# Row maxima of a 16-head attention: 512-key spans for 400-key spans, and the turned maxima split on ScalarE and GpSimd instead of VectorE

## What is computed

```python
def _L0_xattn_ref(values, keys, query, Wv, Wk, Wq, Wo, bo):
    H, Dh = (NUM_HEADS, HEAD_DIM)
    v = (values @ Wv.T).reshape(N, -1, H, Dh)
    k = (keys @ Wk.T).reshape(N, -1, H, Dh)
    q = (query @ Wq.T).reshape(N, -1, H, Dh)
    energy = jnp.einsum('nqhd,nkhd->nhqk', q, k)
    attn = jax.nn.softmax(energy / jnp.sqrt(jnp.float32(EMBED_DIM)), axis=3)
    out = jnp.einsum('nhql,nlhd->nqhd', attn, v).reshape(N, -1, H * Dh)
    return out @ Wo.T + bo
```

## Time and profile before

| | |
|---|---|
| median of three runs | 3645.14 us |
| the profiled execution | 3645.8 us, span 3644.0 us |
| TensorE busy in the span | 3391.9 us (93%) |
| VectorE busy | 2494.9 us (68%) |
| ScalarE busy | 1520.4 us (42%) |
| GpSimd busy | 226.7 us (6%) |
| mean granted TensorE clock | 0.966 of full speed |

### The profile page before, as it was taken

One profiled execution on the slowest core, in us unless ns is written; L12 is line 12 of the kernel. 1 busy time (PEld: TensorE's weight loads), 2 busy tenths in 40 slices (PEclk: granted clock), 3 DMA queues, 4 the chain that ended last, 5 costly groups with the idle time before them and its releaser, 6 DMA issues. The chain is left out here.

```text
span 3644.0 us, 63094 instructions
## 1 busy us (share of the span) xinstructions
PE 3391.9 (93%) x21900; PEld 2020.3 (55%) x21900; DVE 2494.9 (68%) x5808; ACT 1520.4 (42%) x2718; POOL 226.7 (6%) x251
## 2 busy tenths in 40 slices
PE   8979999999999999769977999977999999999999
PEld 5643222222222222258854545546989898989888
DVE  4538888888888888250013444438888888888885
ACT  4534777777777777412211222212222222222221
POOL 0021100000000000030000000000000000000000
PEclk9987999999999999879988999998999999999999
DMA  5687646465554642141120212112000000000000
GB/s 213 240 253 94 82 64 84 67 78 73 74 78 67 85 63 33 52 174 38 37 86 30 90 59 71 60 55 103 9 13 10 12 10 12 10 12 10 12 10 9
DMA packets 144167, 239.79 MB, mean 66 GB/s; under 512 B 22808, under 2 KB 100224, under 8 KB 143488
## 3 DMA queue, kind: packets, MB, share of 16 engines
q1 hardware_dynamic: 134768, 220.67, 28.6%
q0 software_dynamic: 4608, 12.59, 1.1%
q10 hardware_dynamic: 4624, 4.46, 0.4%
HBM read 170.38 MB, written 66.86 MB: 65 GB/s over the span
## 5 line engine op out<-in xcount | busy, mean ns | idle before, releaser
L656 DVE TENSOR_REDUCE at_pmax<-at_psm 128x2 f32<-128x800 f32 (+1 forms) x1024 | 968.1, 986 | 115.8 <-PE at_psm L504 94.0
L597 ACT ACTIVATE ring<-at_pss 128x512 f32<-128x512 f32 (+1 forms) x1664 | 865.2, 600 | 302.6 <-PE at_pss L518 298.3
L518 PE MATMUL at_pss<-at_qs,at_ks 99*128 99x512 bf16 (+1 forms) x1664 | 506.8, 386 | 8.0 <-ACT ring L597 6.5
L1659 PE MATMUL mt_psd<-mt_xl,mt_key_in 128*128 128x128 f32 x4096 | 491.1, 278 | 2.3 <-DMA mt_key_out<-m_out 2.3
L1659 PEld LDWEIGHTS mt_psd<-mt_xl,mt_key_in 128*128 128x128 f32 x4096 | 469.7, 193 | 3.7 <-DMA mt_key_out<-m_out 2.4
L1685 PE MATMUL mt_psu<-mt_key_out,mt_g 128*128 128x256 f32 x2048 | 447.4, 379 | 1.3 <-DVE mt_g L1895 1.3
L526 PE MATMUL at_pso<-ring,at_vw 128*32 128x512 f32 (+1 forms) x3328 | 444.1, 606 | 0.0
L1685 PEld LDWEIGHTS mt_psu<-mt_key_out,mt_g 128*128 128x128 f32 x2048 | 386.7, 190 | 52.6 <-DVE mt_g L1895 1.4
L502 PE MATMUL at_psm<-at_ks,at_qs 64*128 64x400 bf16 (+1 forms) x1024 | 340.1, 347 | 42.6 <-DVE at_pmax L656 18.9
L502 PEld LDWEIGHTS at_psm<-at_ks,at_qs 64*128 64x128 bf16 x1024 | 88.8, 93 | 467.0 <-DVE at_pmax L656 312.7
L504 PE MATMUL at_psm<-at_kh,at_qh 64*128 64x400 bf16 (+1 forms) x1024 | 339.8, 347 | 0.0
(11 more groups left out here) (218 smaller groups left out, 3781.7 us busy)
## 6 DMA issues: line engine op xcount, KB each, us to landing
at_ks<-k_dram SPq DMA_DIRECT2D x192, 200.1 KB, 6.7
k_dram<-pj_kp SPq DMA_DIRECT2D x24, 800.5 KB, 5.5
v_dram<-pj_v SPq DMA_DIRECT2D x8, 1664.0 KB, 9.1
at_vd<-v_dram SPq DMA_DIRECT2D x32, 416.0 KB, 10.7
pj_ctx<-ctxT SPq DMA_DIRECT2D x8, 1601.0 KB, 11.7
at_kh<-k_dram SPq DMA_DIRECT2D x128, 100.1 KB, 5.6
aw_ctxT<-ctxT SPq DMA_DIRECT2D x8, 1601.0 KB, 7.2
at_qs<-q_dram SPq DMA_DIRECT2D x192, 64.0 KB, 7.0
```

What stands on the lines that cost most here:

```text
L518: nc.tensor.matmul(ps_s[0:r, (NST * g + n) % SBANKS, :], ks[:, g, j, kt * P:kt * P + r], qs[:, g, j, :], start=True, stop=True).then_inc(s ...
L597: nc.scalar.activation(pr[0:r, (NST * g + n) % PRING, :], ps_s[0:r, (NST * g + n) % SBANKS, :], ACT.Exp, scale=SCALE).then_inc(expd, 1)
L656: nc.vector.tensor_reduce(pmax[:, 2 * p:2 * p + 2, q, c:c + 1], ps_m[:, n % MBANKS, :, 0:MSPANS[c][1]], AX.X, ALU.max).then_inc(m_red, 1)
L1659: ins = nc.tensor.matmul(ps_d[:, j % 2, y * P:y * P + P], key_in[:, k, j * YB + y, :], xl[:, s, k, :], start=k == 0, stop=k == KC - 1)
```

## The change

- A maxima job takes 512 keys: three full spans per head pair and query tile make 24 jobs. The 65 keys that remain (1536 to 1600) make one job per head pair for all four query tiles: eight matmuls of 65 columns side by side in one double bank, and one reduce of 2 x 4 x 65. That is 26 jobs per unit, exactly two per step.
- The two jobs of a step stand between the second and the third score (`BETWEEN = 2`); there are no third jobs. The two 65-key jobs are the last of a unit, in step 9. Eight jobs (`EARLY`) instead of nine are begun in steps 10 to 13.
- The turn moves to behind the first score of step 10, and the turned maxima go to a bank of the scores' ring `ps_s`: one of every 53 slots of the ring. The scores behind it wait one exponential more, and the third score after it waits for ScalarE's copy of the turned maxima (`m_copied`).
- ScalarE copies the turned maxima to SBUF, behind the first exponential of step 10; GpSimd makes the three bf16 parts from the copy with four instructions, behind `divide` in its order. VectorE's `split` is gone, and with it job 1's wait for `m_parts`.
- `invert`'s pieces stand ahead of jobs 14, 16 and 18 of 26.
- In the beginning: 26 jobs alternate with 26 key products, six key products follow alone, then two jobs of unit 1, the turn, and six more jobs. The bias is loaded ahead of `rows_out`. VectorE's and GpSimd's loops over units are written out.

```diff
-    MSPANS = [(a, n) for a, n in spans(KEYS - 1, 400)]
-    MSPANS = [(0, 401)] + [(a + 1, n) for a, n in MSPANS[1:]]
-    NM = len(MSPANS)
-    max_jobs = [(p, q, c) for p in range(HG // 2) for q in range(QT) for c in range(NM)]
+    MSPAN = 512
+    NFULL, REST = KEYS // MSPAN, KEYS % MSPAN
+    NM = NFULL + 1
+    max_jobs = [(p, q, c) for p in range(HG // 2) for q in range(QT) for c in range(NFULL)]
+    max_jobs += [(p, None, NFULL) for p in range(HG // 2)]
...
-    INVERT_IN, INVERT_AT = 3, (17, 18, 22)
+    INVERT_IN, INVERT_AT = 3, (14, 16, 18)
     TURN_AT = 10
-    THREE = (2, 3, 5, 7, 8, 11, 13)
-    BETWEEN = 3
+    BETWEEN = 2
...
+    def score_slot(u, n):
+
+        return (1 + u * (NST + 1) + n + (n > TURN_BEHIND)) % SBANKS
...
                     pe.wait_ge(m_red, u * NJ + n + 1)
-                    nc.tensor.matmul(ps_m[:, n % MBANKS, 0, 0:w], qs[0:MAX_ROWS, g, 2 * p, q * P:q * P + P],
-                                     ks[0:MAX_ROWS, g, 2 * p, a:a + w], start=True, stop=True)
-                    nc.tensor.matmul(ps_m[:, n % MBANKS, 1, 0:w], qh[MAX_ROWS:2 * MAX_ROWS, g, p, q * P:q * P + P],
-                                     kh[MAX_ROWS:2 * MAX_ROWS, g, p, a:a + w], start=True, stop=True).then_inc(m_mm, 1)
+                    for q, to, w in [(x, x * REST, REST) for x in range(QT)] if q is None else [(q, 0, MSPAN)]:
+                        nc.tensor.matmul(ps_m[:, n % MBANKS, 0, to:to + w], qs[0:MAX_ROWS, g, 2 * p, q * P:q * P + P],
+                                         ks[0:MAX_ROWS, g, 2 * p, a:a + w], start=True, stop=True)
+                        ins = nc.tensor.matmul(ps_m[:, n % MBANKS, 1, to:to + w],
+                                               qh[MAX_ROWS:2 * MAX_ROWS, g, p, q * P:q * P + P],
+                                               kh[MAX_ROWS:2 * MAX_ROWS, g, p, a:a + w], start=True, stop=True)
+                    ins.then_inc(m_mm, 1)
...
                 def turn_max(u):
 
                     pe.wait_ge(m_all, u + 1)
-                    nc.tensor.transpose(turned_at, nmax[:, :], t["ident"][:, :]).then_inc(m_turned, 1)
+
+                    if u:
+                        pe.wait_ge(expd, (u - 1) * NST + TURN_BEHIND + 2)
+                    nc.tensor.transpose(turned_at(u), nmax[:, :], t["ident"][:, :]).then_inc(m_turned, 1)
...
+                    behind = n - TURN_BEHIND
+
+                    if behind == 3:
+                        pe.wait_ge(m_copied, min(u + 2, UNITS))
+                    elif u == 0 and n == 2:
+                        pe.wait_ge(m_copied, 1)
+                    else:
+                        pe.wait_ge(expd, u * NST + n + 1 + (behind in (1, 2)))
...
                         for j in range(HG):
-                            maxima(j, kt)
+                            if j == BETWEEN:
+                                maxima(kt)
                             if kt < KT:
                                 scores(u, g, kt * HG + j)
                             elif nxt is not None:
                                 scores(u + 1, nxt[1], j)
-                        if nxt is not None and kt == TURN_AT:
-                            turn_max(u + 1)
+                            if kt == TURN_AT and j == 0 and nxt is not None:
+                                turn_max(u + 1)
...
+                        if n == TURN_BEHIND and u + 1 < UNITS:
+                            turned_out(u + 1)
...
+                def turned_out(u):
+
+                    act.wait_ge(m_parts, u + 1)
+                    act.wait_ge(m_turned, u + 1)
+                    nc.scalar.activation(mfull[:, :], turned_at(u), ACT.Copy).then_inc(m_copied, 1)
...
+                def split(u):
+
+                    me = Own(pool, own_split, u, 3)
+                    pool.wait_ge(m_copied, u + 1)
+
+                    pool.wait_ge(m_in, u * 48 + 1)
+                    gate(pool, t["pool_gate"])
+                    me.then(nc.gpsimd.tensor_copy(mpart[:, 0, :], mfull[:, :]))
+                    me.then(nc.gpsimd.tensor_tensor(mrest[:, :], mfull[:, :], mpart[:, 0, :], ALU.subtract))
+                    me.then(nc.gpsimd.tensor_copy(mpart[:, 1, :], mrest[:, :]))
+                    nc.gpsimd.tensor_tensor(mpart[:, 2, :], mrest[:, :], mpart[:, 1, :], ALU.subtract).then_inc(m_parts, 1)
```

More of the change, by code:

```diff
@@ L348, in attend_heads, with jobs_at, turn_slot @@
     NLOAD = 2 * len(Q_PART) + 2 * MAX_PARTS
-    INVERT_IN, INVERT_AT = 3, (17, 18, 22)
+    INVERT_IN, INVERT_AT = 3, (14, 16, 18)
     TURN_AT = 10
-    THREE = (2, 3, 5, 7, 8, 11, 13)
-    BETWEEN = 3
+    BETWEEN = 2
     NJ = len(max_jobs)
[L355 to L362, removed]
+    PER_STEP = NJ // KT
+    assert NJ == PER_STEP * KT and QT * REST <= MSPAN
+    EARLY = PER_STEP * (KT + 1 - TURN_AT)
+    TURN_BEHIND = TURN_AT * HG
+    def jobs_at(kt):
+        first = (kt - 1) * PER_STEP + EARLY
+        return [n % NJ for n in range(first, first + PER_STEP)]
+    def score_slot(u, n):
+        return (1 + u * (NST + 1) + n + (n > TURN_BEHIND)) % SBANKS
+    def turn_slot(u):
+        return ((u - 1) * (NST + 1) + TURN_BEHIND + 2) % SBANKS if u else 0
     with Stage(nc, "at") as st:
@@ L541, in unit, with maxima @@
                     nxt, over = ((b, x) if x < G else (b + 1, x - G) if b < last else None for x in (g + 1, g + 2))
-                    def maxima(place, kt):
+                    def maxima(kt):
                         ahead, v = (nxt, u + 1) if kt < TURN_AT else (over, u + 2)
                         if ahead is not None:
-                            for n in plan[kt].get(place, ()):
+                            for n in jobs_at(kt):
                                 max_product(ahead[0], ahead[1], v, n)
@@ L566, in unit @@
                             values(u, g, (kt - 1) * HG + j)
-                        maxima("values", kt)
                 last = B - 1
@@ L572, in _ @@
                     max_product(0, 0, 0, n)
-                max_product(0, 1, 1, 0)
-                turn_max(0)
-                for n in range(1, EARLY):
+                for n in range(NJ, MH * len(halves)):
+                    key_product(n)
+                for n in range(MBANKS):
                     max_product(0, 1, 1, n)
                 pe.wait_ge(k_out, len(halves))
+                turn_max(0)
+                for n in range(MBANKS, EARLY):
+                    max_product(0, 1, 1, n)
                 first_scores(0, 0)
@@ L652, in maxima @@
                             invert(behind, me, INVERT_AT.index(n))
-                        if n == 0 and before is not None:
-                            split(before, me)
+                        if n == 0:
+                            dve.wait_ge(m_all, u)
                         dve.wait_ge(m_mm, u * NJ + n + 1)
-                        nc.vector.tensor_reduce(pmax[:, 2 * p:2 * p + 2, q, c:c + 1], ps_m[:, n % MBANKS, :, 0:MSPANS[c][1]],
-                                                AX.X, ALU.max).then_inc(m_red, 1)
+                        heads, found = pmax[:, 2 * p:2 * p + 2, :, :], ps_m[:, n % MBANKS, :, :]
+                        if q is None:
+                            heads, found = heads[:, :, :, c], found[:, :, 0:QT * REST].rearrange("p j (q n) -> p j q n", n=REST)
+                        else:
+                            heads = heads[:, :, q, c:c + 1]
+                        nc.vector.tensor_reduce(heads, found, AX.X, ALU.max).then_inc(m_red, 1)
                     dve.wait_ge(m_red, (u + 1) * NJ + MBANKS)
+                    dve.wait_ge(m_turned, u)
                     nc.vector.tensor_reduce(nmax[:, :], pmax[:, :, :, :].rearrange("p j q c -> p (j q) c"), AX.X, ALU.max, negate=True).then_inc(m_all, 1)
-                OWN_MAX, OWN = 3, 3 + 2
-                maxima(0, Own(dve, own))
-                maxima(1, Own(dve, own), 0)
-                with dve.Fori(1, UNITS - 1) as u:
-                    me = Own(dve, own, u, OWN)
-                    me.n = OWN_MAX - OWN
-                    maxima(u + 1, me, u, u - 1)
-                me = Own(dve, own, UNITS - 1, OWN)
-                me.n = OWN_MAX - OWN
-                split(UNITS - 1, me)
+                OWN = 2
+                maxima(0)
+                maxima(1)
+                for u in range(1, UNITS - 1):
+                    maxima(u + 1, Own(dve, own, u - 1, OWN), u - 1)
+                me = Own(dve, own, UNITS - 2, OWN)
                 for u in range(UNITS - 2, UNITS):
@@ L720, in _ @@
                 spread(0, 1, False)
+                split(0)
                 add_bias()
-                with pool.Fori(1, UNITS // 2) as i:
+                split(1)
+                for i in range(1, UNITS // 2):
                     for s in range(2):
@@ L725, in _ @@
                         divide(2 * i + s - 2)
+                        split(2 * i + s)
                 for u in range(UNITS - 2, UNITS):
```

30 lines of the change are left out of this document (11 added, 19 removed).

## The result

The changed kernel takes 3562.42 us (median of four runs, 3561.29 to 3567.27) against 3644.63 us for the kernel before beside it. The ratio is 0.9778, 95% interval 0.9761 to 0.9795: 82 us less. Forecast were 3570.7 us, that is 74 less, with a range of 3549 to 3610. The profiled execution is the slowest of the four, 3567.27 us with a span of 3565.6.

The account below looks back on a forecast made before the run. TensorE sets the pace, losing 2.75 us per 37.39 us unit to waits for reduces. 34.02 + 0.02 + 0.2 + 0.72 + 0.05 = 35.0 per unit; -74.4 from 3645.8, median 0.7 lower: 3570.7 us, range 3549 to 3610.

Parts of the forecast that it names:

- The step: TensorE's step of four scores, two jobs and values: 2.617 us, thirteen of them 34.02 us per unit.
- No wait and no reserve: Chain through a bank: 2.85 us from the first job, next step's second job at 2.84, so no ordinary wait, no reserve.
- The rival of a longer chain: Each 1024-column reduce costs 0.05 us more than the slope says: 0.9 us per unit, 3599 us; chance 0.17.
- The 65-key jobs: Small pairs of 65 columns on TensorE: +0.02 us per unit, bounds +0.5 and -0.11 per job.
- The turn: Transpose between two scores on TensorE: 0.2 us per unit, bounded by 0.1 and 0.3.
- The inversion: `invert` on VectorE delays reduces: 0.46 us for the first transpose, 0.26 for the second, together 0.72 per unit.
- The boundary: Step where ScalarE also copies the sums: the fourth score waits for the first's exponential, 0.05 us per unit.
- The beginning: Stretch ahead of the first scores, with its jobs, key products and turn: -1 us, between -4 and +3.
- GpSimd: GpSimd's split of the turned maxima: four instructions of 0.5 us, 2.0 in all, hidden with 1.1 us of cover.
- late rows: GpSimd needs 1.28 us per instruction, so the next unit's first scores wait 2.0 us: 3633 us; chance 0.06.
- VectorE as the bound: Above 1.31 us between reduces, two don't fit a step; at 1.5 us the kernel takes 3703 us; chance 0.05.
- the wait only changes its name: Waits at the second job stay at 2.4 to 2.8 us per unit: 3640 to 3650 us; chance 0.04.

Follow-up runs that it names:

- the memsets: Changed kernel with a dead VectorE memset ahead of each step's second reduce: 3566.86 us with 64 columns, 3600.08 us with 192.
- second run of the changed kernel: The changed kernel itself, unaltered, measured again as base of the follow-ups: 3563.64 us, ratio 0.9778 to the kernel before.
- `BETWEEN = 3`: Changed kernel with each step's two jobs behind the third score instead of the second: 3585.32 us, ratio 0.9829 to the kernel before.
- bunched jobs: Changed kernel with a third job behind the values in steps 2, 5, 11 and one job less in 4, 7, 13: 3662.01 us.
- the run with three memsets: Changed kernel with three dead GpSimd memsets of 1024 columns ahead of each split from the third unit on: 3598.54 us, ratio 0.9874.

## Why the prediction was right, point by point

- **The step**: forecast 2.617, measured 2.61 to 2.64 in steps without extra work. Its terms hold: the second job 0.22 to 0.23 behind the first, the third score 0.31 behind that. It carries the gain, since 26 jobs spaced evenly leave no wait.
- **The reduce**: 1.22 by the slope of the earlier trace rows, measured 1.23; queued ones 2.36 - 1.23 = 1.13 apart, forecast 1.125. The step's idle time on VectorE is 0.26 to 0.35 in ordinary steps, forecast 0.37.
- **No wait and no reserve**: the reserve is shown to be nil by the memsets; in an ordinary step the second reduce ends at 809.66 and the next second job starts at 809.72. The rival of a longer chain had the right price, 0.9 per unit for a chain 0.1 longer (two reduces of 0.05 more), beside 1.18 measured for 0.15; the chain just wasn't longer.
- **The 65-key jobs**: forecast +0.02 per unit, measured -0.09 (step 9 takes 2.53). The truth lies between the nearest row that I took and the lower bound, which for two jobs was -0.22. TensorE's timeline of the changed kernel, the first two small pairs:

```profile
798.90 0.20 PE L511 MATMUL at_psm<-at_ks,at_qs 64*128 64x65 bf16 x1
798.90 0.20 PE L513 MATMUL at_psm<-at_kh,at_qh 64*128 64x65 bf16 x1
798.94 0.19 PE L511 MATMUL at_psm<-at_ks,at_qs 64*128 64x65 bf16 x1
```

  The two matmuls of a pair start together and pairs stand 0.03 to 0.04 apart, where a chain of matmuls that each load 128 rows needs 0.029 for one. But the second job's first pair starts at 799.13, 0.13 behind the last pair of the first job, so that one small job still takes 0.23, as a full one; what the 0.13 are, no run shows. The 0.09 come between the second job and the next score (0.23 instead of 0.32). The rule of the Trainium skill that was weighed there (TensorEngine Tiling, section Tiling Modes, Key Properties), that different tiles work in parallel, agrees with the pairs in these rows; the 7 us that it seemed to promise became 3.
- **The turn**: forecast 0.2, measured 0.11, near the lower bound: I took the middle where a row of it was missing.
- **The inversion**: forecast 0.46 + 0.26, measured 0.38 + 0.17 by the length of steps 5 and 7. The first transpose holds the next reduce up for 0.73 us (820.10 to 820.83) and not 0.83, which is that term's error; for the 0.09 of the second I have no row.
- **The boundary**: forecast 0.05, measured 0.05 (the first scores stand at 811.57 and 814.24, 2.67 apart).
- **Not in the sum**: step 11 is 2.69, 0.07 too long. Its second job starts 0.31 behind the first (804.15, 804.46) and waits for step 10's reduces, which start at 802.04, 0.50 behind their job instead of 0.43.

Together: 13 x 2.62 - 0.09 + 0.11 + 0.55 + 0.05 + 0.07 = 34.75, measured 34.77, forecast 35.0. The 0.23 too much are 7 us over 30 periods: the stretch from the first scores to the last values shrinks from 1193.4 us (316.00 to 1509.38) to 1115.1 in the second run of the changed kernel (317.29 to 1432.39), by 78.3 where 73.4 were forecast.

The forecast of 3570.7 is 8.3 us above the measured median. Of these the stretch explains 4.9, and the beginning, below, takes 2.3 back. Another 2.0 lie behind the attention, which the change doesn't touch (2134.6 us before, 2132.6 in the second run). The rest, some 3.6, is that the profiled execution used here took 3566.72 us and so stands above the medians; the forecast had allowed 0.7 for that. So part of how near the forecast came is luck: errors of both signs met.

- **The beginning**: forecast -1, measured +1.3 (first scores 316.00 before, 317.29). The turn does come earlier, 305.97 against 307.63, as the sum said. What failed is a time that it took as unchanged: the rows' three DMAs land 2.2 us after their issue before and 4.2 after. In the profiled run of the comparison they took 5.9 and the first scores came at 320.43; that is 3 of the 5 us by which this run stands above its median.
- **ScalarE's copy is free**: right, its cover is 0.2 us.
- **The exponential ahead of the third score** was taken to end before the score is due. It does, by 0.1 us, and only because the jobs stand in front. The prediction gave that cover no number, and so I didn't foresee the loss with `BETWEEN = 3`.
- **GpSimd**: forecast 2.0 us for the split, measured 1.62: two copies of 0.28 and two subtractions of 0.42. On VectorE the same four take 0.28, 0.28, 0.22 and 0.28. The rule of the Trainium skill that the prediction weighed (GPSIMD Engine Reference, Performance versus the Vector engine) is 1.96 times slower for an add with two inputs. For the subtractions of this small shape that is too high: 0.42 against 0.28, 1.5 times. The parts are issued at 803.97, 3.1 behind the first score of step 10 instead of 3.4, and the cover is 1.5 to 2.0.
- **The rivals**: late rows need a split over 1.5 us later than it is. VectorE as the bound, with a time above the kernel before, would have needed 1.42 us between reduces, against 1.13. That the wait only changes its name came true in two experiments, not in the change: with the turn and split moved but not the spans, and with bunched jobs.

## What to carry to other kernels

Where one engine feeds another through two buffers, a shorter chain per job isn't the first thing to look for: spread the jobs evenly over the steps first, since with the same work the bunched order was 95 us slower than the even one. Work out the chain through one buffer (start of the job to start of its reader, the reader's queue, its own time, release) and set it against the distance between the jobs that share the buffer; idle time of the reader is no reserve. A change of two parts can be worth more than the parts by themselves (81 us here against 63 and next to nothing), so run each alone, and look in the trace whether a run brings a wait of its own, as both did here. And put an engine's side work where it waits for its input anyway.

## What the runs showed of the hardware that I had not expected

- **The clock fell behind a single wait, and that cost more than the wait.** In the run with three memsets the granted clock went to half after one of the thirty waits, the longest, of 1.83 us; a timeline and a window behind it (columns as above):

```profile
993.45 1.01 PE L539 MATMUL at_pss<-at_qs,at_ks 99*128 99x512 bf16 x2 [1.83 <-issue]
...
996.32 1.94 PE L547 MATMUL at_pso<-ring,at_vw 65*32 65x512 f32 x8
```

```profile
995.00:997.00 2.00, 2.00 (x9) 0.33 (x10) 1.96 (x2) 1.15 (x3) 0.00 (x0) 0.50 0.08 18
```

  Matmuls ran at 1.2 GHz for some 10 us, and two steps took 4.74 and 4.77 us instead of 2.62, so the fall cost more than the wait itself. The wait of 1.52 us shown above had no such effect (clock 1.00 behind it). In the bunched run it happened twice between 400 and 1400 us, behind waits of 1.33 us (the values of 1.56 us in the timeline shown there) and 1.31 us, while a wait of 1.31 us at the same place in another unit (794.09) was followed by values of 1.07 us, so at full clock. What sets it off I can't say from these runs. The changed kernel has clock 1.00 over that whole stretch.
- **A short instruction between two reduces is nearly free.** A memset of 0.11 us between two reduces moved the second's end by 0.03; one of 0.22 us moved it by 0.15.
